# Last attention: odd units turned by a transposing DMA instead of by TensorE, and small products into the unused half of the output bank

## The reference

```
q = _fq_sym(q, axis=-1)
k = _fq_sym(k, axis=-1)
v = _fq_sym(v, axis=2)
attn = jnp.einsum('bhqd,bhkd->bhqk', q, k)
attn = jax.nn.softmax(attn.astype(jnp.float32), axis=-1)
attn = _fq_unsigned(attn, axis=-1)
out = jnp.einsum('bhqk,bhkd->bhqd', attn, v)
```

## Time and profile before

| | before |
|---|---|
| median of 3 runs | 3113.32 us (3108.88 to 3116.57) |
| the profiled execution's own time | 3104.27 us |
| its span, first to last instruction | 3102.4 us |
| mean granted TensorE clock | 0.928 of full |
| PE, DVE, ACT busy in the span | 2480.9, 2111.4, 1629.7 us |
| first to last even exponential of `attend3` | 1805.50 to 2728.83 us |

### The profile page before, as it was taken

One profiled execution on the slowest core, in us unless ns is written; L12 is line 12 of the kernel. 1 busy time (PEld: TensorE's weight loads), 2 busy tenths in 40 slices (PEclk: granted clock), 3 DMA queues, 4 the chain that ended last, 5 costly groups with the idle time before them and its releaser, 6 DMA issues. The chain is left out here.

```text
span 3102.4 us, 51049 instructions
## 1 busy us (share of the span) xinstructions
PE 2480.9 (80%) x19824; PEld 1684.5 (54%) x19848; DVE 2111.4 (68%) x4570; ACT 1629.7 (53%) x2787; POOL 529.9 (17%) x390
## 2 busy tenths in 40 slices
PE   7978999987999454587896667777777777779999
PEld 5755666764666232466565534444444444446666
DVE  6758778764332656575675779999999999942331
ACT  3434555442232444343442468888888888832322
POOL 2114343321221222321221400000000000011211
PEclk9999999998999666899998889999999999989999
DMA  3120000002000210211002220000000000010000
GB/s 132 32 79 7 11 8 11 6 4 82 21 21 11 88 31 7 72 36 44 22 18 85 72 97 15 8 8 15 8 8 15 8 10 14 3 33 11 21 11 11
DMA packets 59023, 92.84 MB, mean 30 GB/s; under 512 B 5521, under 2 KB 54689, under 8 KB 57761
## 3 DMA queue, kind: packets, MB, share of 16 engines
q1 hardware_dynamic: 58784, 89.57, 8.7%
HBM read 66.48 MB, written 23.07 MB: 29 GB/s over the span
## 5 line engine op out<-in xcount | busy, mean ns | idle before, releaser
L2353 ACT ACTIVATE attend_ex<-psum,attend_mx,queries_step 128x1024 uint16<-128x1024 f32 x512 | 618.4, 1208 | 125.4 <-DVE attend_mx L2384 125.4
L2453 PEld LDWEIGHTS psum<-ident_b,attend_ex 128*128 128x128 bf16 x4096 | 249.1, 100 | 399.0 <-issue 397.9
L2453 PE MATMUL psum<-ident_b,attend_ex 128*128 128x128 bf16 x4096 | 325.0, 224 | 154.8 <-DVE attend_pw L2388 123.7
L2441 PE MATMUL psum<-keys_turned,attend_qt 96*128 96x512 bf16 x1024 | 322.2, 398 | 86.4 <-ACT attend_ex L2353 75.1
L1274 PE MATMUL psum<-arena,moe_tokT 128*128 128x512 f32 (+2 forms) x896 | 361.5, 548 | 0.0
L2377 DVE TENSOR_REDUCE attend_mx<-psum 128x1 f32<-128x512 f32 x512 | 329.3, 685 | 26.0 <-PE psum L2441 7.6
L2373 DVE TENSOR_REDUCE attend_mx<-psum 128x1 f32<-128x1024 f32 x256 | 310.8, 1214 | 14.3 <-PE psum L2441 14.1
L1189 DVE TENSOR_TENSOR moe_h<-moe_sg,psum 128x512 f32<-128x512 f32 (+1 forms) x112 | 69.9, 625 | 273.6 <-PE psum L1274 265.6
L1274 PEld LDWEIGHTS psum<-arena,moe_tokT 128*128 128x128 f32 x896 | 166.4, 192 | 136.0 <-issue 121.1
L1050 ACT ACTIVATE moe_sg<-psum 128x512 f32<-128x512 f32 (+1 forms) x112 | 61.4, 548 | 297.3 <-PE psum L1274 293.1
L2463 PE MATMUL psum<-values,attend_pw 128*128 128x16 f16 x4096 | 180.0, 170 | 1.4 <-DVE attend_pw L2388 0.6
(11 more groups left out here) (420 smaller groups left out, 4784.1 us busy)
## 6 DMA issues: line engine op xcount, KB each, us to landing
queries_turned<-qkv_qT SPq DMA_DIRECT2D x16, 384.0 KB, 3.1
attend_qt<-queries_turned SPq DMA_DIRECT2D x16, 384.0 KB, 3.3
arena<-in_moe SPq DMA_DIRECT2D x1, 5704.0 KB, 18.4
arena<-in_gqa SPq DMA_DIRECT2D x1, 5440.0 KB, 18.7
arena<-in_moe SPq DMA_DIRECT2D x1, 4360.0 KB, 13.7
xatt_ct<-in_ctx_T SPq DMA_DIRECT2D x32, 128.0 KB, 2.2
residual<-xatt_y SPq DMA_DIRECT2D x32, 128.0 KB, 2.0
moe_xt<-residual SPq DMA_DIRECT2D x16, 256.0 KB, 3.0
```

Source lines behind the costliest of these rows:

```text
L2353: nc.scalar.activation(ex[:, u % 4], S[:, u % 3], ACT.Exp, bias=mx[:, t % 2, h, 4:5], scale=steps[:, 0, t, h:h + 1], accum_out=sums[:, t % ...
L2441: last = nc.tensor.matmul(S[:, u % 3, b * 512:(b + 1) * 512], qt[:, t % 2, h * P:(h + 1) * P], KT[:, c:c + 4, h // 2], start=True, stop=True)
L2453: last = nc.tensor.transpose(TP[:, c], counts[u % 4][:, c * P:(c + 1) * P], k["ident_b"][:])
```

## The change

Odd units are no longer turned by TensorE. SyncE issues, for each odd unit, one transposing DMA from `ex[:, u % 4]` to `pw[:, u % 4]`, after the exponential of u and attend of u - 4. attend(u) and exp(u + 4) of odd units wait for its landing. Even units are turned as before; of their copies ScalarE makes three in four and VectorE one in four (where u of its pair is a multiple of 8; it copies u - 2). A function `keep_clock` puts three products of 256 columns by an identity into `IDLE`, the other half of bank 7, behind each attend, except at one unit per batch. Because both halves of the bank are now written within one accumulation, each batch begins with a product of zeros that opens the whole bank, and all products of attend accumulate. The load of the next phase's weights is issued from ScalarE's queue, and a batch's store stands in SyncE's queue in the middle of the next batch.

```diff
@@ SyncE
+            def turn(u):
+                sp.wait_ge(s["exped"], u + 1)
+                if u >= 4:
+                    sp.wait_ge(s["attended"], u - 3)
+                sp.dma_start_transpose(out=pT[u % 4], in_=ex[:, u % 4].bitcast(F16)).then_inc(s[f"landed{u % 4}"], 16)
...
-            start_next(sp, s["weights_next"])
-            for t in range(B):
-                if t + 2 < B:
+            for u in range(1, NU, 2):
+                t, at = u // UN, u % UN
+                turn(u)
+                if at == UN - 1 and t + 2 < B:
                     load(t + 2)
-                store(t)
+                if t and at == 15:
+                    store(t - 1)
+            store(B - 1)
@@ ScalarE
-                if u >= 4:
-                    act.wait_ge(s["turned"], u - 3)
+                if u >= 4 and u % 2 == 0:
+                    act.wait_ge(s["turned"], u // 2 - 1)
+                if u >= 4 and u % 2:
+                    act.wait_ge(s[f"landed{u % 4}"], u // 4 * 16)
...
+            load_next[0](act, s["weights_next"])
             for u in range(0, NU, 2):
                 exp(u)
-                if u >= 2:
+                if u >= 2 and (u - 2) % 8 != 6:
                     evacuate(u - 2)
                 exp(u + 1)
-            evacuate(NU - 2)
@@ VectorE
                 maximum(u + 1)
                 bias(u + 1)
-                if u >= 4:
-                    evacuate(u - 3)
+                if u >= 2 and (u - 2) % 8 == 6:
+                    evacuate(u - 2)
...
-            evacuate(NU - 3)
+            evacuate(NU - 2)
             row_steps(B - 1)
-            evacuate(NU - 1)
@@ TensorE
             def turn(u):
                 pe.wait_ge(s["exped"], u + 1)
-                if u >= 1:
-                    pe.wait_ge(s["evacuated"], u)
+                if u >= 2:
+                    pe.wait_ge(s["evacuated"], u // 2)
...
             def attend(u):
                 t, h = u // UN, u % UN // 2
-                pe.wait_ge(s["evacuated"], u + 1)
+                if u % 2 == 0:
+                    pe.wait_ge(s["evacuated"], u // 2 + 1)
+                else:
+                    pe.wait_ge(s[f"landed{u % 4}"], (u // 4 + 1) * 16)
                 if t and u % UN == 0:
                     pe.wait_ge(s["scaled"], t)
+                if u % UN == 0:
+                    nc.tensor.matmul(k["psum"][:, 7, :], zero[:], KT[:, 0:4, 0], start=True, stop=False)
...
+            def keep_clock():
+                for c in range(KEEP):
+                    nc.tensor.matmul(IDLE, k["ident_b"][0:W3], KT[:, c:c + 2, 0], start=False, stop=False)

             for u in range(NU + LAG + 1):
                 if u < NU:
                     score(u)
-                if LAG <= u < NU + LAG:
+                if LAG <= u < NU + LAG and u % 2 == 0:
                     turn(u - LAG)
                 if u > LAG:
                     attend(u - LAG - 1)
+                if u > LAG and (u - LAG) % UN:
+                    keep_clock()
```

More of the change, by code:

```diff
@@ L2297, in attend3 @@
     LAG = 4
+    KEEP = 3
     LN255 = 5.541263545158426
@@ L2305, in attend3 @@
             even_scores odd_scores unit_max row_max bias exped turned evacuated
-            attended both row_recip probs_step scaled o_done""")
+            attended both row_recip probs_step scaled o_done landed1 landed3 zeroed""")
         S = k["psum"][:, 0:6, :].rearrange("p (u b) c -> p u (b c)", b=2)
@@ L2310, in attend3 @@
         O = k["psum"][:, 7, 0:D]
+        IDLE = k["psum"][:, 7, D:2 * D]
         qt = sb("qt", [W3, 2, NH * P], BF16)
@@ L2317, in attend3 @@
         o = sb("o", [P, 2, D])
+        zero = sb("zero", [W3, P], BF16)
         counts = [ex[:, r].bitcast(BF16) for r in range(4)]
@@ L2331, in store @@
                 sp.dma_start(out[t], o[:, t % 2]).then_inc(s[f"o_stored{t % 2}"], 16)
-            start_next, finish_next = load_next
             load(0)
             load(1)
-            start_next(sp, s["weights_next"])
-            for t in range(B):
-                if t + 2 < B:
+            for u in range(1, NU, 2):
+                t, at = u // UN, u % UN
+                turn(u)
+                if at == UN - 1 and t + 2 < B:
                     load(t + 2)
-                store(t)
+                if t and at == 15:
+                    store(t - 1)
+            store(B - 1)
             for j in range(2):
                 sp.wait_ge(s[f"o_stored{j}"], B // 2 * 16)
-            finish_next(sp, s["weights_next"])
+            load_next[1](sp, s["weights_next"])
         @block.scalar
@@ L2356, in evacuate @@
             def evacuate(u):
-                act.wait_ge(s["turned"], u + 1)
+                act.wait_ge(s["turned"], u // 2 + 1)
                 nc.scalar.copy(pw[:, u % 4], TPW).then_inc(s["evacuated"], 1)
+            load_next[0](act, s["weights_next"])
             for u in range(0, NU, 2):
                 exp(u)
-                if u >= 2:
+                if u >= 2 and (u - 2) % 8 != 6:
                     evacuate(u - 2)
                 exp(u + 1)
-            evacuate(NU - 2)
         @block.vector
@@ L2386, in evacuate @@
             def evacuate(u):
-                dve.wait_ge(s["turned"], u + 1)
+                dve.wait_ge(s["turned"], u // 2 + 1)
                 nc.vector.tensor_copy(pw[:, u % 4], TPW).then_inc(s["evacuated"], 1)
@@ L2424, in _ @@
                     scale_columns(t - 1)
-            evacuate(NU - 3)
+            evacuate(NU - 2)
             row_steps(B - 1)
-            evacuate(NU - 1)
             scale_rows(B - 1)
             scale_columns(B - 1)
+        @block.gpsimd
+        def _(pool):
+            nc.gpsimd.memset(zero[:], 0.0).then_inc(s["zeroed"], 1)
         @block.tensor
         def _(pe):
+            pe.wait_ge(s["zeroed"], 1)
             def score(u):
@@ L2463, in attend @@
                     last = nc.tensor.matmul(O[:, h * HD:(h + 1) * HD], pT[u % 4][:, c], V[:, kc, h * HD:(h + 1) * HD],
-                                            start=kc == 0, stop=kc == B - 1)
+                                            start=False, stop=u % UN == UN - 1 and c == UC - 1)
                 last.then_inc(s["attended"], 1)
+            def keep_clock():
+                for c in range(KEEP):
+                    nc.tensor.matmul(IDLE, k["ident_b"][0:W3], KT[:, c:c + 2, 0], start=False, stop=False)
             for u in range(NU + LAG + 1):
```

## The result

| | before | after |
|---|---|---|
| median | 3112.45 us (4 runs, 3108.88 to 3116.57) | 3153.36 us (4 runs, 3146.73 to 3157.97) |
| span of the profiled execution | 3102.4 us | 3149.9 us |
| first to last even exponential | 923.3 us | 961.4 us (1814.89 to 2776.3) |

The account below looks back on a forecast made before the run. The 3.54 us ring bounds the kernel, VectorE's queue almost level. 902.7 + 33.4 + 3.0 = 939.1 against 923.3 is +15.8, about 2 more for the start; 3104.3 + 17 = 3121, timed median 9 above: 3130, range 3118 to 3142.

Parts of the forecast that it names:

- The ring of 3.54: Round of one pair (even exponential, odd score, two maxima, bias, next even exponential): 3.54 us, no copy or transpose on it.
- The stall: At 63 places VectorE's copy of u-2 waits for TensorE's turn, delaying the odd maximum 0.53 us each: 33.4 us.
- The fastest rival: TensorE turns u-2 before VectorE comes to copy it, so only the gains are left: 3096 us, chance 0.12.
- The batch boundaries: Pairs lengthened once per batch by VectorE's row steps and output scaling: 0.88 us, 15 times, 13.2 us; 3.0 remain.
- the clock term: TensorE, about as busy with the small products, keeps its higher clock, winning up to 7.4 us.
- The sum 939.1: Stage from first to last even exponential, clock always higher: 902.7 + 33.4 + 3.0 us, against 923.3 before.
- The start: Start of the stage, clock low and weights' load running beside the first transposing DMAs: about 2 us more.
- The transposing DMA: 256 KB for odd units, taken to land 4.2 us from the exponential's end, hidden; rival of landing late, chance 0.26.
- The bound of 6.4: Upper estimate of the transposing DMA's landing: 1,024 packets, 64 an engine, 4.7 us, plus 1.7 of the shortest transfer.
- eight blocks in turn: Rival: one DMA's blocks go one after another, 10.5 us by the skill's page; at 13.6, about 5,680 us, chance 0.06.
- the point of 4.9: Transposing DMA's landing, from the end of its exponential, above which attend delays the odd score: 4.9 us.
- The clock falling for good: Rival: TensorE's clock falls to 1.2 GHz and stays; 4.28 us a pair, 168 us more, near 3281, chance 0.06.

Follow-up runs that it names:

- e1: Changed kernel with ScalarE making every copy of an even unit and VectorE none inside the loop: 3100.5 us, ratio to before 0.9962.
- e10: Changed kernel with ScalarE making all copies, KEEP = 2 and the even unit's exponential split in two halves: 3102.2 us, ratio to before 0.9960.
- e2: Changed kernel with VectorE's one copy in four moved behind the next pair's first maximum: 3121.2 us, ratio to before 1.0022.
- e5: Changed kernel with KEEP = 4 small products instead of three, stalled pairs left: 3167.9 us, ratio to before 1.0178.
- e6: Changed kernel with ScalarE making all copies and KEEP = 2 small products: 3100.7 us, ratio to before 0.9959.
- e9: Changed kernel, stalled pairs left, with seven more small products in one unit of eight, except where a batch begins: 3144.4 us, ratio to before 1.0094.
- e8: Changed kernel with ScalarE making all copies and the next phase's weights loaded in the phase before, from SyncE's queue: 3104.3 us, ratio to before 0.9967.
- e3: Changed kernel with ScalarE issuing the weights' load only after both first query loads have landed: 3158.4 us, ratio to before 1.0143.
- e4: Changed kernel with KEEP = 0, no small products: 3212.3 us, ratio to before 1.0320.
- e12: Changed kernel with ScalarE making all copies, KEEP = 3 and the even unit's exponential split in two halves: 3094.7 us, ratio to before 0.9943.

## Why the prediction was right in kind and short in size

The forecast was 3130 with 3118 to 3142 as its own range; 3153.4 lies above that, inside the wide range of 3098 to 3235. The order of events on the engines came out as worked out; one term of the sum did not.

- **The ring of 3.54** held to the hundredth in every kernel that left its links alone, with VectorE freed of 0.60 (e1). That a second ring of 3.29 lay close behind it was not seen; it changes nothing in this change, and it spoilt the forecast for e10.
- **The stall** was right in place, cause and size: 0.53 forecast, pairs of 4.07 measured, 0.45 of it gone when the copy stands one place later (e2). The fastest rival, that it doesn't come, is refuted by the 0.61 of idle.
- **The batch boundaries** won what was worked out in their second pair (3.67 and not 4.27). The third, 3.69 before without the lower clock, takes 3.54 in e1, but 3.76 to 4.70 in the changed kernel, where the clock falls.
- **The step that failed is the clock term**: "with them it is about as busy, so I expect the higher clock to be kept, and to win up to the 7.4 us above". TensorE was about as busy on average, as said, and the clock fell nonetheless, on the gap of 1.1 us that the stalled pair opens and on that of 1.6 us at the boundary, where no product stands. The sum 939.1 had nothing for it, and the stage took 961.4, 22.3 more. Behind the third pair, what the pairs take above their length at the higher clock (4.07 stalled, 3.67 for the second of a batch, 3.54) adds up to 21.0 us: that is what the term measured. The first three pairs add 2.6, and the boundaries give back 1.0. In the kernel before the same count is 6.4 us, so **the clock cost three times as much as before, where it was to cost nothing**. A microsecond at the lower level costs about the same in both (21.0 us for 145, 6.4 for 55); there are more of them. With more products the price does rise: e5 loses 36.6 us in 140. e1, e6 and e9 tie the fall to the gaps; that a gap does it and not the work per pair is shown by e5 and e9 together. It does not follow every gap: there are 63 stalled places and 35 low stretches, and what decides among them stays open.
- **The start** was put at 2 us; it is 3.8 for the queries' load beside the weights', and a further 1.6 in the third pair (5.72 against 4.16 before), 5.4 together. Both go with the weights' load (in e8, without it, the third pair takes 3.97), and neither e3 nor e8 won the time back.
- **The transposing DMA** was taken at 4.2 from the end of the exponential and measured 3.1 from its issue in the median, 3.0 to 4.8 but for the first: hidden, at its slowest by little. The bound of 6.4 had the packets right and their price wrong: the queue has 1,055 packets more for each transposing DMA, but they took about 0.025 us each (22.2% of 16 engines' 3149.9 us for 328,976 packets, against 8.7% of 3102.4 us for 58,784) and not 0.073. The estimate from the Trainium skill's page "DMA: Bandwidth & Descriptors", section "Latency and other measured facts" (1.0 us of transfer), goes better with the 3.1 than that bound. By the table of the Trainium skill's page "VectorE: DVE Perf Modes", section "The three transpose paths", eight blocks in turn are 10.5 us, by the prediction's estimate; this trace refutes that adding up, as a DMA of eight blocks landed in 3.1. In the changed kernel the point of 4.9 from which it costs was passed only where the weights' load ran beside it; it was not tried by itself.
- **The clock falling for good** did not happen; e4 shows what it would have cost.

## What to carry to other kernels

Before an engine is relieved, walk round the ring of semaphores once and add it up, then look for the next ring behind it: relieving an engine beside the ring gains nothing, and a copy put one place too early in its queue puts its wait on the ring. When work is taken from TensorE, look at the longest gap that is left and not at the average share: filler products belong into that gap first. Spread evenly while it is left, they cost (e5); with no such gap left, one more in every unit helped (e12). A DMA moved to another queue still shares the engines with what was meant to go first.

## What was not expected of the hardware

- A transposing DMA of 256 KB from SBUF to SBUF lands 3.1 us after its issue in the median (178 of 256 within 3.3, the others up to 4.8), like a plain one of that size, while its issue holds SyncE's queue for 1.23 us. Beside a 5.7 MB load it took 7.4 in the changed kernel and 12.9 in e3.
- TensorE's granted clock stayed at 0.93 with 496 products more (e5) and was 0.99 with 496 fewer and no stalls (e6).
- An exponential of 512 columns takes 0.77 from its start to the next one's, and two take 1.52 to the copy behind them (e10), where one of 1,024 takes 1.20: splitting costs 0.32.
